# A graph layer with batch and layer norm on one core: another bank for the second half's product, the edges behind x and the weights, one group's low parts by VectorE, high parts two a tile

## The chip, the core and the metric

The kernel runs on one core of a Trainium2 chip. The metric is the device time of one execution in microseconds (us). Before the change three runs took 2590.15, 2593.97 and 2595.03 us, median 2593.97. TensorE (PE) multiplies, its weight loads are listed apart as PEld; VectorE is DVE, ScalarE is ACT, GpSimd is POOL, and SyncE (SP) issues most of the transfers.

## The reference, cut to what matters

x has 50000 rows of 512 numbers; `src` and `dst` list 75000 edges, sorted by `dst`, with every row's loop to itself among them.

```python
summed = segment_sum(x[src], dst, n)
cnt = segment_sum(ones, dst, n)
aggr = summed / maximum(cnt, 1)[:, None]
h = aggr @ W_l.T + b_l + x @ W_r.T
mu = mean(h, axis=0); var = mean(square(h - mu), axis=0)
y = x + relu((h - mu) * rsqrt(var + EPS) * gamma + beta)
out = (y - mean(y, -1)) / sqrt(var(y, -1) + EPS)
```

Since each row has its loop, the kernel computes h as x (W_l + W_r) plus z, where z is the mean over a row's edges of (x of the source minus x of the row), times W_l. Only some rows have edges beside the loop.

## The kernel before, in words

The rows of x come in 78 groups of five tiles of 128 rows (`TG` = 5) and a last one of 80 rows. There are two phases. Phase one computes h, writes it to memory (`h_scratch`) and sums its columns and their squares. Phase two reads h and x again, normalises, and writes `out`.

**A group in phase one.** SP loads the turned x of a group (`raw`, two buffers). The load of group g+2 is issued when PE has finished group g (`after_group`, L377). Each fp32 number is split in two parts, so that three products of reduced precision give the accuracy of fp32: ACT writes the high part (`x_high`, L728, four pieces kc = 0 to 3), POOL or DVE the low part by a subtraction (`x_low`, L1309 on POOL, L1045 on DVE). PE multiplies a tile in 12 matmuls (`product`, L524 to L526) into one of the two banks `pd0`, `pd1`, which take turns. ACT copies a finished tile out of its bank (`copy_h`, L735). So tile t+2 can't begin before tile t is copied.

**The front.** The first 8 groups (`FRONT` = 8) have nothing but plain tiles for PE, while DVE works out from the edges which rows need a correction. PE makes seven sorts of small sums for this between its tiles (the table `between`): `rank_extras` after tile (6, 2), `sum_cover` after (7, 1). Only then is `s_flag` set, which tells every engine whether the edges are of the usual kind. POOL makes all the low parts of the front. In ACT's order a front tile's copy is followed by one piece of the high part of the next group (L766 and on: copy 0, piece 0, copy 1, piece 1 and so on). The first piece waits for `raw`.

**The turns.** Then come 84 turns (u = -2 to 81). Those from 0 to 77 mix a correction for about 256 rows (in two halves h = 0, 1 of 128) with four or five plain tiles; 351 tiles are left for the turns, and the last three corrections have none beside them. PE's order in a turn: spread 0, tile, spread 1, tile, turn 0, tile, turn 1, tile, z of half 0, a fifth tile in about half of the turns, `fill_slots` (23 small matmuls for the turn after next), z of half 1. "Turn h" transposes the differences `dd` into bank `turned[h]`, px for half 0 and p7 for half 1 (`transpose_difference`, L621). ACT and DVE write high and low part from there (`difference_high` L786, `difference_low` L1100), PE multiplies them by W_l into the one bank pz (`correction`, `times_wl`, L627 to L629), ACT copies z to `zz` (`copy_z`, L793), and POOL adds it to `h_scratch` by an indirect transfer (L1379) and then gathers the rows of x for the turn after (L1331). DVE begins the differences when the gathered rows land (L1079). In ACT's and DVE's order stand also the squares and sums of a group three turns back (L799, L1109, L1116).

Each engine works through its own list in order; semaphores tie them together. The wait that guards pz: half 1 of turn u waits for `s_ze` 2u+1, the copy of half 0 just before it.

**The start.** SP issues x of group 0, both weights, x of group 1, three short vectors and a clearing store. ACT issues six small loads of the edges (L745 to L757) on its own queue, before its first activation. PE's first matmul needs the low part of W_l + W_r, which DVE and ACT make once both weights are there (L926, L762, L922).

## Time and profile before

| | |
|---|---|
| runs, us | 2590.15, 2593.97, 2595.03 |
| the profiled execution, us | 2596.68, of which the span of its instructions 2594.9 |
| busy: PE, DVE, ACT, POOL | 1757.6, 1956.6, 1471.8, 1456.2 us |
| mean granted TensorE clock | 0.845 of full speed |
| front, start to the first tile of group 8 | 0 to 156 us |
| turns | 156 to 1840 us |
| last sums and the norm's vectors | to 1883 us |
| phase two | 1883 to 2595 us |

How to read it: times in the rows are microseconds from the span's start. In a timeline row stand start, duration, engine, line, operation, what it writes and reads, how often it is repeated, and in brackets how long the engine was idle before it and what ended that. A merged row (x4) gives the duration of all four. In a row of waits stand who waited for whom, the total, the number and the longest. PE at full clock issues a matmul of 512 columns each 0.23 us, so that a tile takes 2.72 us.

### The profile page before, as it was taken

The page shows a single profiled execution, that of the slowest core. Times are in us where ns is not written, and L with a number is a line of the kernel's source. Part 1 is how long each engine was busy: PE and PEld are TensorE (multiplying, and loading weights), DVE is VectorE, ACT ScalarE, POOL GpSimd, SP SyncE. Part 2 cuts the span into 40 slices and gives each one's busy share as a digit, 9 for nine tenths or more (in the row PEclk, how much of TensorE's full clock was granted, in tenths as well). Part 3 has the DMA queues.
Part 4 walks back from the last instruction along what each step waited for, and adds up shares of the span by engine and source line. Part 5 has one row for each costly group of instructions (what it writes and reads, how often), then busy time and mean ns, then how long its engine had stood idle before and what let it go on. Part 6 is the DMA issues. An engine that isn't in the chain of part 4 may idle for free.

```text
span 2594.9 us, 29629 instructions
## 1 busy us (share of the span) xinstructions
PE 1757.6 (68%) x9404; PEld 1415.7 (55%) x9404; DVE 1956.6 (75%) x3451; ACT 1471.8 (57%) x2847; POOL 1456.2 (56%) x700
## 2 busy tenths in 40 slices
PE   7899999999999999999999999996400000000000
PEld 5778778878877887787778778874200000000000
DVE  6745878888877888888788888785688666666666
ACT  4333455545554554454445445542389988888887
POOL 5354555555555555555565555554196655555564
PEclk9999999999999999999999999997755555555555
DMA  5466878887888878888788878877599999999998
GB/s 184 139 211 206 260 250 266 277 253 246 257 263 255 258 246 259 258 255 264 234 262 271 255 243 253 280 240 247 163 410 426 426 426 426 426 412 414 421 421 344
DMA packets 125533, 752.89 MB, mean 290 GB/s; under 512 B 20809, under 2 KB 20809, under 8 KB 65726
## 3 DMA queue, kind: packets, MB, share of 16 engines
q1 hardware_dynamic: 70464, 617.84, 62.1%
q0 software_dynamic: 53664, 132.51, 20.7%
q8 instruction: 77, 1.26, 0.2%
q10 hardware_dynamic: 1246, 0.60, 0.1%
q14 instruction: 82, 0.67, 0.1%
HBM read 515.32 MB, written 246.22 MB: 293 GB/s over the span
## 4 chain that ended last, share of the span: by engine, by line
PE 33%; DMA 32%; issue 9%; DVE 9%; ACT 8%; POOL 7%; SPq 0%; POOLq 0%; ACTq 0%; DVEq 0%
DMA out<-hx 19%; PE pd L524 7%; PE pd L526 7%; PE pd L525 7%; DMA xn<-x,gi 5%; DMA xf<-x,gi 5%; PE pz L627 3%; PE pz L629 3%; PE pz L628 3%; ACT hx L881 3%; POOL xn L1331 2%; ACT hx L891 2%; DVE x_lo L1045 2%; POOL xf L1331 2%; DMA hs<-h_scratch 1%
## 5 line engine op out<-in xcount | busy, mean ns | idle before, releaser
L524 PE MATMUL pd<-wc_hi,x_hi 128*128 128x512 f32 x1564 | 628.8, 402 | 34.8 <-DVE wc_lo L922 17.3
L1379 POOL DMA_INDIRECT h_scratch<-zz,si x156 | 308.8, 1979 | 564.5 <-ACT zz L793 506.9
L735 ACT ACTIVATE h_out<-pd 128x512 f32<-128x512 f32 x391 | 233.6, 597 | 672.3 <-PE pd L526 652.1
L526 PE MATMUL pd<-wc_hi,x_lo 128*128 128x512 f32 x1564 | 614.6, 393 | 0.0
L525 PE MATMUL pd<-wc_lo,x_hi 128*128 128x512 f32 x1564 | 612.9, 392 | 0.0
L1402 POOL TENSOR_TENSOR hx<-hx,scale_b 128x2560 f32<-128x2560 f32 (+2 forms) x91 | 439.4, 4838 | 293.3 <-DMA hx<-h_scratch 251.8
L524 PEld LDWEIGHTS pd<-wc_hi,x_hi 128*128 128x128 f32 x1564 | 295.4, 189 | 98.5 <-issue 29.9
L526 PEld LDWEIGHTS pd<-wc_hi,x_lo 128*128 128x128 f32 x1564 | 295.2, 189 | 64.7
L525 PEld LDWEIGHTS pd<-wc_lo,x_hi 128*128 128x128 f32 x1564 | 295.9, 189 | 57.9
L1331 POOL DMA_INDIRECT xn<-x,gi x156 | 264.9, 1698 | 47.7 <-issue 47.7
L881 ACT ACTIVATE hx<-hx,nm 128x512 f32<-128x512 f32 x391 | 277.1, 710 | 2.8
L891 ACT ACTIVATE hx<-hx,nr,rs 128x512 f32<-128x512 f32 x385 | 278.6, 798 | 0.0
L627 PE MATMUL pz<-wl_hi,dT_hi 128*128 128x512 f32 x624 | 256.5, 411 | 28.9 <-ACT zz L793 20.3
L1331 POOL DMA_INDIRECT xf<-x,gi x156 | 248.7, 1594 | 47.6 <-issue 47.3
L1079 DVE SCALAR_TENSOR_TENSOR xf<-xn,ndeg,xf 128x512 f32<-128x512 f32 x156 | 114.9, 746 | 185.8 <-issue 140.3
L799 ACT ACTIVATE hs<-hs 128x512 f32<-128x512 f32 x391 | 219.1, 621 | 51.1 <-DVE acc L1109 51.1
L628 PE MATMUL pz<-wl_lo,dT_hi 128*128 128x512 f32 x624 | 247.4, 396 | 0.0
L629 PE MATMUL pz<-wl_hi,dT_lo 128*128 128x512 f32 x624 | 246.4, 395 | 0.0
L728 ACT ACTIVATE x_hi<-raw 128x640 fp32r<-128x640 f32 (+1 forms) x316 | 214.1, 724 | 40.7 <-DMA raw<-xT_whole 40.6
L1109 DVE TENSOR_TENSOR acc<-acc,hs 128x2560 f32<-128x2560 f32 (+1 forms) x79 | 220.1, 2786 | 21.7 <-DMA hs<-h_scratch 21.7
L1116 DVE TENSOR_TENSOR acc<-acc,hs 128x2560 f32<-128x2560 f32 (+1 forms) x79 | 220.2, 2787 | 16.0 <-ACT hs L799 16.0
L1045 DVE TENSOR_TENSOR x_lo<-raw,x_hi 128x640 fp32r<-128x640 f32 x280 | 209.4, 808 | 14.7 <-ACT x_hi L728 14.7
(221 smaller groups left out, 2855.0 us busy)
## 6 DMA issues: line engine op xcount, KB each, us to landing
raw<-xT_whole SPq DMA_DIRECT2D x78, 1280.0 KB
h_scratch<-h_out SPq DMA_DIRECT2D x78, 1280.0 KB
hs<-h_scratch SPq DMA_DIRECT2D x78, 1280.0 KB
hx<-x SPq DMA_DIRECT2D x78, 1280.0 KB, 20.7
hx<-h_scratch SPq DMA_DIRECT2D x77, 1280.0 KB, 15.4
out<-hx SPq DMA_DIRECT2D x77, 1280.0 KB, 18.0
xn<-x,gi POOLq DMA_INDIRECT x156
xf<-x,gi POOLq DMA_INDIRECT x156
```

The costliest lines, as they stand in the source:

```text
L524: pe.matmul(pd[i][0:n, :], hi, wc["hi"][:, kc, :], start=kc == 0, stop=False)
L525: pe.matmul(pd[i][0:n, :], hi, wc["lo"][:, kc, :], start=False, stop=False)
L526: last = pe.matmul(pd[i][0:n, :], lo, wc["hi"][:, kc, :], start=False, stop=kc == KC - 1)
L627: pe.matmul(out_bank[0:n, :], hi, wl["hi"][:, kc, :], start=kc == 0, stop=False)
L628: pe.matmul(out_bank[0:n, :], hi, wl["lo"][:, kc, :], start=False, stop=False)
L629: last = pe.matmul(out_bank[0:n, :], lo, wl["hi"][:, kc, :], start=False, stop=kc == KC - 1)
L881: act.activation(hb[i][0:n, t, :], xb[i][0:n, t, :], ACT.Square, bias=nm2[0:n, k % 4, t:t + 1], accum_out=ssq2[0:n, k % 4, t:t + 1]).then_ ...
L891: act.activation(hb[i][0:n, t, :], xb[i][0:n, t, :], ACT.Identity, bias=nr2[0:n, k % 4, t:t + 1], scale=rs2[0:n, k % 4, t:t + 1]).then_inc ...
L1045: dve.tensor_tensor(x_lo[:, b, kc, 0:n], raw[:, b, kc, 0:n], x_hi[:, b, kc, 0:n].bitcast(F32), ALU.subtract).then_inc(s_xld, 1)
L1331: return pool.indirect_dma_start(out=table if scatter else out, out_offset=by if scatter else None, in_=out if scatter else table, in_offs ...
L1379: pool.indirect_dma_start(out=h_dram[:, :], out_offset=by, in_=zz[:, h, :], in_offset=None, bounds_check=N + 2 * P - 1, oob_is_err=True, c ...
L1402: pool.tensor_tensor(hb[i][0:n, a:b], hb[i][0:n, a:b], scale_b[0:n].unsqueeze(1).to_broadcast([n, b - a, D]), ALU.mult).then_inc(s_mul, 1)
```

## The change

Four edits, with new places for two small steps that hang on the third.

1. The z of half 1 is written to px (`z_to`), which by then has been read by ACT and DVE. Half 1 has no wait for a copy any more, half 0 waits for the copy of half 0 of the turn before, and the transposition of half 0, which writes px, waits for the copy of half 1 of the turn before.
2. The six small loads of the edges are issued by SP, after both weights and ahead of x of group 1.
3. The low parts of group 4 (`MIDDLE`) are made by DVE in the midst of its work on the edges, not by POOL. `rank_extras` stands after tile (5, 3) and `sum_cover` after (6, 1).
4. In the front two pieces of the high part follow each of the copies 0 and 1, instead of one piece each of the copies 0 to 3.

```diff
+MIDDLE = 4
...
+        z_to = (pz, px)
...
         def lo_by_dve(g):
-            return KC * g - KC * FRONT + 1
+            return KC * g - KC * FRONT + KC + 1
+        def lo_by_pool(g):
+            return KC * g + KC - KC * (g > MIDDLE)
...
+            sp.dma_start(src_i[:, :, 0:EB], src.rearrange("(c b p) -> b c p", b=BP, p=EB)).then_inc(s_src, 16)
...
+            sp.wait_ge(s_pad, 1)
+            sp.dma_start(dst_i[:, 1:BC - 1, 0:wide], blocks(BP, [[EB, BP], [lot, BC - 2]])).then_inc(s_dst, 16)
...
             load_xT(1)
...
                 if t == 0:
-                    if isinstance(g, int) and g <= FRONT:
-                        pe.wait_ge(s_xlp, KC * g + (KC if g > 0 else 1))
+                    if isinstance(g, int) and g == MIDDLE:
+                        pe.wait_ge(s_xld, KC + 1)
+                    elif isinstance(g, int) and g <= FRONT:
+                        pe.wait_ge(s_xlp, lo_by_pool(g) if g > 0 else 1)
...
-                (6, 2): (rank_extras,),
-                (7, 1): (sum_cover,),
+                (5, 3): (rank_extras,),
+                (6, 1): (sum_cover,),
...
                 if u > 0:
                     pe.wait_ge(s_dl, 2 * u + h - 1)
+                    if h == 0:
+                        pe.wait_ge(s_ze, 2 * u)
...
                 pe.wait_ge(s_dl, 2 * u + h + 1)
-                if 2 * u + h > 0:
-                    pe.wait_ge(s_ze, 2 * u + h)
-                times_wl(pz, P, h).then_inc(s_z, 1)
+                if h == 0 and u > 0:
+                    pe.wait_ge(s_ze, 2 * u - 1)
+                times_wl(z_to[h], P, h).then_inc(s_z, 1)
...
-                    if g >= 1 and t < KC:
-                        x_high(g + 1, (g + 1) % 2, t)
+                    if g >= 1 and t < KC // 2:
+                        for kc in (2 * t, 2 * t + 1):
+                            x_high(g + 1, (g + 1) % 2, kc)
...
-                act.activation(zz[:, h, :], pz[:], ACT.Copy, scale=wgt[:, u % 4, h:h + 1]).then_inc(s_ze, 1)
+                act.activation(zz[:, h, :], z_to[h][:], ACT.Copy, scale=wgt[:, u % 4, h:h + 1]).then_inc(s_ze, 1)
...
                 dve.scalar_tensor_tensor(vals[a, :, :, k], v, 256.0, vd, ALU.subtract, ALU.mult)
+            for kc in range(KC):
+                x_low(MIDDLE, MIDDLE % 2, kc)
             for k, v in enumerate((dlo, slo)):
...
-            for g in range(1, FRONT):
-                for kc in range(KC):
-                    x_low(g + 1, (g + 1) % 2, kc)
+            for g in range(2, FRONT + 1):
+                for kc in range(KC if g != MIDDLE else 0):
+                    x_low(g, g % 2, kc)
```

The order of ACT before, in groups 0 (its last copies) and 1 of the front (h_out is a tile's copy, x_hi a piece of the next group):

```order
L735 ACTIVATE h_out<-pd 128x512 x2
L728 ACTIVATE x_hi<-raw 128x640
L735 ACTIVATE h_out<-pd 128x512
L728 ACTIVATE x_hi<-raw 128x640
L735 ACTIVATE h_out<-pd 128x512
L728 ACTIVATE x_hi<-raw 128x640
L735 ACTIVATE h_out<-pd 128x512
L728 ACTIVATE x_hi<-raw 128x640
```

and in the changed kernel, at the same place:

```order
L761 ACTIVATE h_out<-pd 128x512 x2
L754 ACTIVATE x_hi<-raw 128x640 x2
L761 ACTIVATE h_out<-pd 128x512
L754 ACTIVATE x_hi<-raw 128x640 x2
L761 ACTIVATE h_out<-pd 128x512 x4
```

Two pieces, not one, stand ahead of the copy of tile 1, and none between the copies of tiles 1 (after its two) and 4.

DVE before, in the work on the edges during group 3 (vals are what the slots are filled from):

```order
L997 TENSOR_TENSOR e_c<-e_a,e_c 125x780
L999 SCALAR_TENSOR_TENSOR vals<-got,e_d 125x780 x2
L1001 TENSOR_TENSOR vals<-got,e_d 125x780 x2
L1002 CAST vals<-e_act 125x780
```

and in the changed kernel:

```order
L1017 TENSOR_TENSOR e_c<-e_a,e_c 125x780
L1019 SCALAR_TENSOR_TENSOR vals<-got,e_d 125x780 x2
L926 TENSOR_TENSOR x_lo<-raw,x_hi 128x640 x4
L1023 TENSOR_TENSOR vals<-got,e_d 125x780 x2
L1024 CAST vals<-e_act 125x780
```

The four subtractions of group 4 have come in between.

SP at the start of the changed kernel (before, L356 for group 1 followed the two weights at once):

```order
L365 DMA raw<-xT_whole 128x2560
L370 DMA w_raw<-wT_l 128x4x512
L370 DMA w_raw<-wT_r 128x4x512
L371 DMA src_i<-src 120x5x125
L379 DMA dst_i<-dst 120x3x127
L380 DMA dst_i<-dst 119x127
L381 DMA dst_i<-dst 119x127
L382 DMA dst_i<-dst 1x126
L383 DMA dst_i<-dst 1x126
L365 DMA raw<-xT_whole 128x2560
```

The load of group 1's x has moved behind six small ones, on the same queue.

## Rows read from the trace of the kernel before

**Rows 1.** Windows of the core: busy PE, PEld, DVE, ACT, POOL; clock, DMA share, GB/s.
```profile
156.00:1750.00 1594.00, 1559.52 (x8541) 1264.16 (x8541) 1270.43 (x1838) 777.87 (x1342) 895.05 (x527) 1.00 0.81 255
...
1883.00:2595.00 712.00, 0.00 (x0) 0.00 (x0) 507.81 (x1416) 595.57 (x1333) 439.10 (x91) 0.50 0.99 414
```

**Rows 2.** Timeline of the start, ACT, DVE and PEld.
```profile
6.62 1.28 ACT L728 ACT_TABLE_LOAD   x1 [6.62 <-issue]
15.08 1.29 DVE L926 TENSOR_TENSOR w_raw<-w_raw 128x512 f32<-128x512 f32 x2 [11.63 <-DMA w_raw<-wT_r]
17.27 0.29 PEld L524 LDWEIGHTS pd<-wc_hi,x_hi 128*128 128x128 f32 x1 [17.27 <-issue]
19.53 2.61 ACT L728 ACTIVATE x_hi<-raw 128x640 fp32r<-128x640 f32 x4
20.74 0.81 DVE L935 CAST srcf<-src_i 120x625 f32<-120x625 int32 x1 [0.39 <-DMA dst_i<-dst]
```

**Rows 3.** DMA, 0 to 33 us: a queue's packets, MB, share; an issue's us to landing.
```profile
q10 hardware_dynamic: 1246, 0.60, 7.6%
...
w_raw<-wT_r SPq DMA_DIRECT2D x1, 1024.0 KB, 13.2
```

**Rows 4.** Timelines round group 4's first tile (DVE's x_lo: a turn); one window last.
```profile
87.17 0.60 ACT L735 ACTIVATE h_out<-pd 128x512 f32<-128x512 f32 x1 [1.49 <-PE pd L526]
98.94 0.60 ACT L735 ACTIVATE h_out<-pd 128x512 f32<-128x512 f32 x1 [11.17 <-PE pd L526]
...
93.42 0.29 PEld L524 LDWEIGHTS pd<-wc_hi,x_hi 128*128 128x128 f32 x1 [6.71 <-POOL x_lo L1309]
...
80.92 12.44 POOL L1309 TENSOR_TENSOR x_lo<-raw,x_hi 128x640 fp32r<-128x640 f32 x4 [19.31 <-ACT x_hi L728]
...
117.97 4.64 POOL L1309 TENSOR_TENSOR x_lo<-raw,x_hi 128x640 fp32r<-128x640 f32 x3 [7.69 <-ACT x_hi L728]
...
76.83 5.47 DVE L999 SCALAR_TENSOR_TENSOR vals<-got,e_d 125x780 bf16<-125x780 f32 x2
...
1010.49 3.02 DVE L1045 TENSOR_TENSOR x_lo<-raw,x_hi 128x640 fp32r<-128x640 f32 x4
...
94.00:99.50 5.50, 5.50 (x15) 4.29 (x13) 5.47 (x9) 0.56 (x2) 0.00 (x0) 0.51 0.46 193
```

**Rows 5.** Timelines of groups 5 to 8, ACT, PEld, POOL; waits of PEld, 17 to 156.
```profile
110.13 0.60 ACT L735 ACTIVATE h_out<-pd 128x512 f32<-128x512 f32 x1 [1.49 <-PE pd L526]
...
117.15 0.74 ACT L728 ACTIVATE x_hi<-raw 128x640 fp32r<-128x640 f32 x1 [3.17 <-DMA raw<-xT_whole]
117.80 0.58 ACT L735 ACTIVATE h_out<-pd 128x512 f32<-128x512 f32 x1
...
124.31 0.60 ACT L735 ACTIVATE h_out<-pd 128x512 f32<-128x512 f32 x1 [1.49 <-PE pd L526]
...
118.43 0.19 PEld L524 LDWEIGHTS pd<-wc_hi,x_hi 128*128 128x128 f32 x1
...
146.95 9.01 POOL L1309 TENSOR_TENSOR x_lo<-raw,x_hi 128x640 fp32r<-128x640 f32 x4 [6.96 <-ACT x_hi L728]
...
156.01 0.19 PEld L524 LDWEIGHTS pd<-wc_hi,x_hi 128*128 128x128 f32 x1 [2.08 <-POOL x_lo L1309]
...
PEld pd L524 <- POOL x_lo L1309: 9.4, 4, 6.7
```

**Rows 6.** The chain that ended last, 235 to 1750 us, by line; PEld's waits there.
```profile
by line: issue 14.1%; DMA xn<-x,gi 9.2%; PE pd L524 8.9%; PE pd L526 8.8%; PE pd L525 8.8%; DMA xf<-x,gi 7.8%; PE pz L627 5.0%; PE pz L629 4.5%; PE pz L628 4.5%; POOL xn L1331 4.0%; DVE x_lo L1045 3.3%; POOL xf L1331 2.8%; DVE hot L1051 1.8
...
PEld pz L627 <- issue: 16.2, 33, 1.6
```

**Rows 7.** Timelines: half 1's copy and the next transposition; the last turn's z.
```profile
479.18 0.67 ACT L793 ACTIVATE zz<-pz,wgt 128x512 f32<-128x512 f32 x1
...
484.95 0.37 PEld L621 LDWEIGHTS px<-ident,dd 128*128 128x128 f32 x2
...
1835.15 0.19 PEld L627 LDWEIGHTS pz<-wl_hi,dT_hi 128*128 128x128 f32 x1 [1.27 <-issue]
```

More of the change, by code:

```diff
@@ L361, in _, with blocks @@
                 sp.dma_start(w_raw[:, m], w.rearrange("(c p) f -> p c f", p=P)).then_inc(s, 16)
+            sp.dma_start(src_i[:, :, 0:EB], src.rearrange("(c b p) -> b c p", b=BP, p=EB)).then_inc(s_src, 16)
+            wide, lot = EB + 2, BP * EB
+            def blocks(first, pattern):
+                return bass.AP(dst.tensor, first * EB - 1, [*pattern, [1, wide]])
+            sp.wait_ge(s_pad, 1)
+            sp.dma_start(dst_i[:, 1:BC - 1, 0:wide], blocks(BP, [[EB, BP], [lot, BC - 2]])).then_inc(s_dst, 16)
+            sp.dma_start(dst_i[1:BP, 0, 0:wide], blocks(1, [[EB, BP - 1]])).then_inc(s_dst, 16)
+            sp.dma_start(dst_i[0:BP - 1, BC - 1, 0:wide], blocks((BC - 1) * BP, [[EB, BP - 1]])).then_inc(s_dst, 16)
+            sp.dma_start(dst_i[0:1, 0, 1:wide], dst[0:EB + 1].rearrange("(o p) -> o p", o=1)).then_inc(s_dst, 16)
+            sp.dma_start(dst_i[BP - 1:BP, BC - 1, 0:wide - 1], dst[E - EB - 1:E].rearrange("(o p) -> o p", o=1)).then_inc(s_dst, 16)
             load_xT(1)
@@ L510, in product @@
                 if t == 0:
-                    if isinstance(g, int) and g <= FRONT:
-                        pe.wait_ge(s_xlp, KC * g + (KC if g > 0 else 1))
+                    if isinstance(g, int) and g == MIDDLE:
+                        pe.wait_ge(s_xld, KC + 1)
+                    elif isinstance(g, int) and g <= FRONT:
+                        pe.wait_ge(s_xlp, lo_by_pool(g) if g > 0 else 1)
                     else:
-                        pe.wait_ge(s_xlp, KC * FRONT + KC)
+                        pe.wait_ge(s_xlp, lo_by_pool(FRONT))
                         pe.wait_ge(s_xld, lo_by_dve(g))
@@ L743, in copy_window @@
                                    banks[a % 3][j][0:EB, 0:HALF], ACT.Copy).then_inc(s_got, 1)
-            act.dma_start(src_i[:, :, 0:EB], src.rearrange("(c b p) -> b c p", b=BP, p=EB)).then_inc(s_src, 16)
-            wide, block = EB + 2, BP * EB
-            def blocks(first, pattern):
-                return bass.AP(dst.tensor, first * EB - 1, [*pattern, [1, wide]])
-            act.wait_ge(s_pad, 1)
-            act.dma_start(dst_i[:, 1:BC - 1, 0:wide], blocks(BP, [[EB, BP], [block, BC - 2]])).then_inc(s_dst, 16)
-            act.dma_start(dst_i[1:BP, 0, 0:wide], blocks(1, [[EB, BP - 1]])).then_inc(s_dst, 16)
-            act.dma_start(dst_i[0:BP - 1, BC - 1, 0:wide], blocks((BC - 1) * BP, [[EB, BP - 1]])).then_inc(s_dst, 16)
-            act.dma_start(dst_i[0:1, 0, 1:wide], dst[0:EB + 1].rearrange("(o p) -> o p", o=1)).then_inc(s_dst, 16)
-            act.dma_start(dst_i[BP - 1:BP, BC - 1, 0:wide - 1], dst[E - EB - 1:E].rearrange("(o p) -> o p", o=1)).then_inc(s_dst, 16)
             for kc in range(KC):
@@ L907, in link, with x_low @@
                 dve.wait_ge(s, steps[s])
+            def x_low(g, b, kc):
+                n = LAST if isinstance(g, int) and g == G else GR
+                dve.wait_ge(s_xh, KC * g + kc + 1)
+                dve.tensor_tensor(x_lo[:, b, kc, 0:n], raw[:, b, kc, 0:n], x_hi[:, b, kc, 0:n].bitcast(F32),
+                                  ALU.subtract).then_inc(s_xld, 1)
             dve.memset(dst_i[0:1, 0, 0:1].bitcast(F32), -1.0)
@@ L1040, in _ @@
             dve.memset(psl[:], 0.0).then_inc(s_ct, 1)
-            def x_low(g, b, kc):
-                n = LAST if isinstance(g, int) and g == G else GR
-                dve.wait_ge(s_xh, KC * g + kc + 1)
-                dve.tensor_tensor(x_lo[:, b, kc, 0:n], raw[:, b, kc, 0:n], x_hi[:, b, kc, 0:n].bitcast(F32),
-                                  ALU.subtract).then_inc(s_xld, 1)
             def one_hots(u):
```

## The prediction

> **What bounds the kernel now.** I read the windows first, to see which engine fills which stage. In the turns PE is busy 1559.5 of 1594 us at full clock; in phase two PE does nothing and DMA is busy 0.99 of the time [rows 1]. Phase two moves the same bytes after the change as before, so it is a block of 712 us that only starts earlier or later. What the change is worth must therefore be read from PE's idle time before 1883 us, and from the end of that stage. Next the waits of PEld (the weight load is the first thing that a stalled PE does not do), which name the two places: 9.4 us for POOL's x_lo in the front [rows 5] and 16.2 us in 33 waits ahead of half 1's z in the turns [rows 6]. Last the chain of waits, which tells whether time won at such a place reaches the end. Between 235 and 1750 us only about 43% of it is PE (26.5% plain tiles, 14% z, small rest); the gathers of xn and xf alone are 17%, and POOL's issuing of them another 7% [rows 6]. So PE is nearly full and yet not the only thing on the path: two chains of about the same length run side by side.
>
> **Part 1, the start (edit 2).** PE's first load is at 17.27, 2.2 us after DVE gets the second weight at 15.08; ACT's table load begins at 6.62, when ACT has issued its last edge load, though nothing it needs is late [rows 2]. The weight takes 13.2 us from issue to landing, and the edges' queue puts 1246 small packets for 7.6% of 33 us, that is 2.5 us of all 16 engines, among the packets of x and weights [rows 3]. About nine tenths of them come before the weight lands; behind it on one queue they cost it nothing, so the weight and with it PE come 2.3 us earlier. The edges land later but have slack: DVE is free for them at 20.35 (20.74 less 0.39 idle) [rows 2], which becomes 18.0. What is late next is x of group 1, now behind the edges. Before, ACT took it up at 19.53 without waiting [rows 2]; with 3.5 us of transfer behind 2.5 us of edges I put it at 19.3 where 17.2 is wanted. Its four pieces (2.61 us) stand in ACT's queue ahead of the copy of tile (0, 0), and PE's third tile waits for that copy: I take 0.5 us. Sum -1.8. From both sides: -3.3 (weights 2.8 earlier and half a microsecond from ACT's table load) to +1.5 (x of group 1 three microseconds late). The Trainium skill, "DMA: Bandwidth & Descriptors", section "Why a DMA increments its semaphore by 16 and not by 1", says that a transfer uses the largest number of engines up to 16 that divides its slowest dimension; for the two loads of 119 rows that is 7 engines, with 34 packets each, against 15 if spread over all. At 32 ns a packet (2.5 us x 16 / 1246) x of group 1 would then come 0.6 us later and the term would be -1.2; no row of this trace tells which engine took what.
>
> **Part 2, group 4 (edit 3).** POOL's four subtractions for group 4 take 12.44 us, against 1.55 each (4.64 for three) where DVE isn't at work on the same memory; DVE's L999 beside them takes 5.47 for two [rows 4]. PE stands 6.7 us, and then runs the tile's rest at half speed: the granted clock from 94 to 99.5 is 0.51 [rows 4]. From one copy to the next pass 98.94 - 87.17 = 11.77 us instead of 2.72: 9.05 us lost in one tile. After the change DVE does the four in 3.02 us [rows 4], POOL does nothing then, and both causes go. The high parts are there by 83.5, so DVE is done by 84.5, and PE wants them at about 87: slack 2.5 us. I take -9.05; the bounds are -9.1 and -6 (if DVE came 3 us too late). DVE's own work is 3 us longer, but L999 and what follows no longer share with POOL, so the marks for `rank_extras` come no later than now; moved to tile (5, 3) it asks for them some 5 us after they are ready.
>
> **Part 3, the front's other groups (edits 3 and 4).** Let T be the end of a group as ACT's copy shows it, which is also when the load of the next x but one is issued. In rows 5 T = 110.13; the first high piece starts at T+7.0 (117.15), the copy of tile 1 at T+7.7 (117.80), PE's fourth tile at T+8.3 (118.43), just when that copy has ended, and the group ends at T+14.2 (124.31). So the fourth tile of a group is already tied to the load. With two pieces ahead of the copy it comes 0.65 us later: fourth tile at T+8.95, end at T+14.8, where five tiles need 13.6. Low parts: first at T+7.8, four of 1.55 us, done at T+14.1, in time. Thus the pairs take away the wait for x_lo at a group's start (0.66 us in rows 5) and put one of about 1.1 us ahead of its fourth tile. I count groups 2 to 6: 5.0 us in all. Then there is the place of the flag. With `sum_cover` after (7, 1), DVE's one-hot tables run beside the low parts of group 8, which take 9.01 us for 6.2 [rows 5]. With it after (6, 1) they run beside those of group 7: +2.8 us, done at T+16.9 where PE wants them at 14.5, a wait of 2.4 us. Against this go the old waits, 9.4 - 6.7 = 2.7 us, and 2.08 us at 156.01 [rows 5]. Sum +2.6; bounds -4.8 (nothing new waits) and +5 (clock at half rate after the 2.4 us wait, which costs up to 1.6 more, and rank_extras late).
>
> **Part 4, the turns (edit 1).** Half 1's z waits in 33 turns, 16.2 us in all, because copy and issue lie between two products in the same bank [rows 6]. This wait goes altogether. What can be late instead: the transposition of half 0 now waits for the copy of half 1 of the turn before. In rows 7 that copy ends at 479.85, the transposition begins at 484.95: 5.1 us of slack, two plain tiles. Behind it on PE would stand everything, so it matters only if it is passed. What is late next is the differences: POOL gathers after adding the turn's last z, 9 to 12 us later DVE can go on, and this loop does not know of pz. Where it is on the chain, a z done sooner only lengthens PE's next wait for DVE. So I take the share of the chain that is PE's, 0.43 of 16.2 = -7.0. Bounds: 0 (all given back) and -17.8 (all kept, and one fall of the clock, 1.6 us, behind the longest wait of 1.6 us saved).
>
> **Part 5, the last turns.** There no tile stands between the halves; the last z of half 1 begins after 1.27 us of waiting at 1835.15 [rows 7], and the last addition, sums and statistics hang on it. -1.2, bounds 0 and -1.6.
>
> **Sum.** -1.8 - 9.05 + 2.6 - 7.0 - 1.2 = -16.4 us. The profiled execution took 2596.7 us (span 2594.9 and 1.8 around it), so 2580.3; it stands 2.7 us above the median of the three runs shown, 2594.0. Against the median I predict 2577.5 us. A change of 0.2% is 5.2 us, about the least that a measurement of this kernel can tell from none.
>
> **The rivals.**
> *The front alone pays.* In the turns the gathers are the bound, part 4 gives 0, the start gives 0.5. For it: the gathers' share of the chain, and that all but the longest of the 33 waits are short, 0.49 us on average, less than the jitter of a gather. Against: PE is busy 98% of the stage. Time: -0.5 - 9.05 + 2.6 - 1.2 = -8.2, 2586.
> *All waits saved are kept, and the pairs cost nothing.* PE's fourth tile finds its copy in time since x lands sooner with PE earlier. -2.5 - 9.05 - 2 - 13 - 1.2 = -27.8, 2566. Against it: the fourth tile is tied to the copy to 0.1 us already [rows 5].
> *The transposition waits (the slower side).* Copy_z of half 1 stands in ACT's list behind the squares of an older group, which wait for DVE's sum, which waits for a load. If this copy came over 5.1 us later than in rows 7 in most turns, PE would stop in all of the 78 turns at a place where it never did. The point from which it decides is 5.1 + 16.4/78 = 5.3 us late; at 5.5 us late 0.4 x 78 = 31 us against 16.4: 2609. For it: ACT's list is in order, and PE now arrives sooner. Against: in rows 7, an instance with squares before the copy, the slack is still 5.1.
> *Group 4 is not repaired:* DVE comes to its four subtractions only after PE wants them, or PE waits as long for the marks at (5, 3). Then part 2 gives 3 instead of 9: 2583 to 2590, within 0.2% only together with part 4 at zero.
>
> **Chances.** Forecast (2571 to 2584) 0.50; front alone (2583 to 2588) 0.22; all kept (2563 to 2571) 0.15; group 4 not repaired 0.08; transposition waits 0.05. Faster by over 0.2% 0.88, within 0.2% 0.07, slower by over 0.2% 0.05. The range for 8 in 10 leaves out the slow rival and the outer part of the two bounds: 2564 to 2589.
>
> **What would show it.** Start: PEld's first load at about 15.0, and ACT's first copy some 0.5 us behind PE's tile. Group 4: no gap near 87 us, clock 1.00 through the front, DVE's four low parts at 3.0 us. Pairs: a wait of PEld for the copy (`h_out`) ahead of fourth tiles, about 1 us in five groups; one wait for x_lo of about 2.4 us at group 7, none at 8; the first tile of group 8 at about 148. Turns: no wait ahead of half 1's z; the waits for DVE's dd and dT_lo larger by some 9 us together; phase two beginning near 1866. I am wrong if waits of PEld appear ahead of the transposition for ACT's zz, if group 4 still waits, or if the turns are not shorter by at least 3 us.

## The result, and the profile after

| Kernel | median us | lowest to highest | runs | against before | 95% interval |
|---|---|---|---|---|---|
| before | 2594.45 | 2590.15 to 2603.87 | 11 | 1 | |
| changed | 2585.88 | 2578.47 to 2589.50 | 11 | 0.9965 | 0.9952 to 0.9977 |

The change makes the kernel 0.35% faster, 8.6 us, with an interval of 6.0 to 12.4 us. Forecast were 16.4 us. The side is right and the time lies in the range, but half of the gain is missing. The changed kernel was timed once more beside the last experiments: 0.9957 (0.9940 to 0.9973), 2585.66 us. The profile of the changed kernel that is read below took 2589.41 us, span 2587.6.

Windows of the changed kernel (busy us of PE, PEld, DVE, ACT and POOL with instruction counts, clock, DMA share, GB/s). The first two answer to [rows 1]; the others are two places in the front that the text comes to below:
```profile
156.00:1750.00 1594.00, 1560.03 (x8584) 1265.86 (x8584) 1274.08 (x1849) 781.92 (x1351) 886.81 (x527) 1.00 0.81 255
1883.00:2587.00 704.00, 0.00 (x0) 0.00 (x0) 502.50 (x1405) 592.45 (x1324) 431.99 (x85) 0.50 0.99 414
...
99.40:102.80 3.40, 3.40 (x10) 2.61 (x9) 3.37 (x3) 1.10 (x2) 3.40 (x3) 0.51 0.00 0
133.50:136.90 3.40, 3.40 (x10) 2.65 (x9) 0.60 (x1) 0.76 (x2) 3.40 (x2) 0.52 0.00 0
```
Phase two is the block that it was (712.4 us before, 712.2 now, from the norm's scale to the end). So the gain must lie ahead of it. A stage is best timed by one recurring instruction; I used the start of ACT's copy of a group's last tile, the first transposition of a turn, and the moment at which the scale for phase two is ready:

| us from the span's start | before | changed | gained so far |
|---|---|---|---|
| group 0 ends | 32.89 | 31.91 | 1.0 |
| group 3 ends | 87.17 | 88.31 | -1.1 |
| group 4 ends | 110.13 | 106.21 | 3.9 |
| group 5 ends | 124.31 | 121.54 | 2.8 |
| group 6 ends | 139.12 | 139.56 | -0.4 |
| group 9 ends | 184.24 | 184.87 | -0.6 |
| turn 0 transposes | 190.86 | 191.48 | -0.6 |
| turn 74 transposes | 1759.66 | 1753.58 | 6.1 |
| scale ready | 1882.55 | 1875.45 | 7.1 |

This is the main reading: the front, from which 8.3 us were expected, gave nothing, and the turns with the last turns gave 7.7, where 8.2 were expected. It is read from one profile of each kernel; how far one profile can be trusted is said ahead of the experiments.

The start, changed kernel (start, us, engine, line, operation, what ended the idle time before it); it answers to [rows 2]:
```profile
0.82 1.28 ACT L754 ACT_TABLE_LOAD   x1 [0.82 <-PEq L1445]
3.19 3.21 SPq L379 DMA_DIRECT2D dst_i<-dst  x1
6.44 2.29 SPq L380 DMA_DIRECT2D dst_i<-dst  x1
15.37 0.29 PEld L548 LDWEIGHTS pd<-wc_hi,x_hi 128*128 128x128 f32 x1 [15.37 <-issue]
```
And the DMA issue of the weight in the first 33 us (KB, us to landing), which answers to [rows 3]:
```profile
w_raw<-wT_r SPq DMA_DIRECT2D x1, 1024.0 KB, 10.8
```
The weight lands in 10.8 instead of 13.2 us and PE begins 1.9 us earlier. Only 1.0 of it is left at the end of group 0. SP itself is busy issuing the edges' loads till 10.44, 5.5 us with two of them, and x of group 1 is issued behind that, at 10.49.

Group 4's first tile, changed kernel, DVE and then ACT; it answers to [rows 4]:
```profile
77.22 5.46 DVE L1019 SCALAR_TENSOR_TENSOR vals<-got,e_d 125x780 bf16<-125x780 f32 x2
82.38 3.14 DVE L926 TENSOR_TENSOR x_lo<-raw,x_hi 128x640 fp32r<-128x640 f32 x4
85.42 5.47 DVE L1023 TENSOR_TENSOR vals<-got,e_d 125x780 bf16<-125x780 f32 x2
...
88.31 0.60 ACT L761 ACTIVATE h_out<-pd 128x512 f32<-128x512 f32 x1 [2.12 <-PE pd L550]
91.03 0.60 ACT L761 ACTIVATE h_out<-pd 128x512 f32<-128x512 f32 x1 [2.12 <-PE pd L550]
```
The repair works: the low parts are there at 85.5, and one copy follows the other by 2.72 us where it was 11.77. DVE's pair at 77.22 takes 5.46 us with POOL idle, and took 5.47 before; but before, it started at 76.83 and POOL's subtractions only at 80.92, so it ran beside them for its last 1.4 us only. The pair that did run beside POOL before is the next one, L1001:
```profile
82.01 7.75 DVE L1001 TENSOR_TENSOR vals<-got,e_d 125x780 bf16<-125x780 f32 x2
```
It took 7.75 us where the changed kernel, with POOL idle, needs 5.47 (L1023). So both engines suffered: POOL's four subtractions took 12.44 us, and DVE lost 2.3 on this pair.

What went wrong is five tiles later. ACT, then PEld, changed kernel, the load of group 5 and PE's fourth tile of group 4; the last row is group 6's fourth tile, with the load of group 7 ([rows 5] has the same places of before):
```profile
96.92 1.36 ACT L754 ACTIVATE x_hi<-raw 128x640 fp32r<-128x640 f32 x2 [5.29 <-DMA raw<-xT_whole]
98.19 0.58 ACT L761 ACTIVATE h_out<-pd 128x512 f32<-128x512 f32 x1
...
98.82 0.19 PEld L548 LDWEIGHTS pd<-wc_hi,x_hi 128*128 128x128 f32 x1 [2.81 <-ACT h_out L761]
...
132.18 0.19 PEld L548 LDWEIGHTS pd<-wc_hi,x_hi 128*128 128x128 f32 x1 [2.55 <-ACT h_out L761]
```
x of group 5 lands 8.6 us after group 3 ended, not 7.0. The pair of high parts and the copy behind it come that much later; PE stands 2.8 us, and 0.7 us after it goes on its clock falls to half for 3.4 us (0.51 in the window from 99.40 above): ten matmuls, where the stretch from 103.0 to 106.4, at full clock, has 16. The same happens at 132.

The largest wait of PEld in the front (17 to 190 us), changed kernel (us in total, times, longest):
```profile
PEld pd L548 <- ACT h_out L761: 10.9, 7, 2.8
```
All seven end before 156 us, the end of the window in [rows 5]; in that window 9.4 us for x_lo have become 10.9 us for the copy.

The turns, changed kernel, 235 to 1750 us: the chain that ended last by line, then the waits of PEld; they answer to [rows 6]:
```profile
by line: issue 13.8%; DMA xf<-x,gi 9.6%; PE pd L548 8.7%; PE pd L550 8.6%; PE pd L549 8.6%; DMA xn<-x,gi 6.4%; POOL xn L1347 4.9%; DVE x_lo L926 3.4%; POOL xf L1347 3.2%; PE pz L653 2.8%; PE pz L654 2.5%; PE pz L655 2.5%; PE px L653 2.1%; P
...
PEld pd L548 <- issue: 17.1, 15, 2.5
PEld px L647 <- DVE dd L1110: 13.4, 11, 2.0
PEld p L647 <- DVE dd L1110: 11.7, 16, 0.8
PEld pz L653 <- DVE dT_lo L1116: 7.9, 20, 0.7
PEld pe L637 <- DVE xe_lo L1100: 7.3, 7, 1.2
```
The wait ahead of half 1's z is gone and there is none for `zz`. The other five were 12.2, 9.9, 11.0, 8.6 and 3.4 us before: they grew by 12.3 us together. The share of PE in the chain is what it was, and the gathers stand on it as before.

### The profile page after: what moved, and what is told of

Read it like the earlier page. It is cut to its first block, busy times and chain, and to the rows that moved or that the text cites. A ratio compares the mean times of both kernels' runs of the same rounds, so it can differ in the third digit from the quotient of the medians.

```text
span 2587.6 us, 29551 instructions
## 1 busy us (share of the span) xinstructions
PE 1753.3 (68%) x9404; PEld 1413.6 (55%) x9404; DVE 1955.3 (76%) x3455; ACT 1471.5 (57%) x2847; POOL 1434.7 (55%) x696
## 4 chain that ended last, share of the span: by engine, by line
DMA 35%; PE 33%; issue 9%; DVE 8%; ACT 7%; POOL 7%; SPq 1%; POOLq 0%; DVEq 0%; ACTq 0%
DMA out<-hx 21%; PE pd L548 7%; PE pd L550 7%; PE pd L549 7%; DMA xf<-x,gi 6%; DMA xn<-x,gi 4%; POOL xn L1347 3%; DMA raw<-xT_whole 2%; ACT hx L895 2%; DVE x_lo L926 2%; POOL xf L1347 2%; PE pz L653 2%; ACT hx L905 2%; PE pz L654 2%; PE pz L655 2%
## 5 line engine op out<-in xcount | busy, mean ns | idle before, releaser
L1347 POOL DMA_INDIRECT xn<-x,gi x156 | 278.3, 1784 | 47.7 <-issue 47.4
L1347 POOL DMA_INDIRECT xf<-x,gi x156 | 235.5, 1510 | 47.5 <-issue 47.5
L926 DVE TENSOR_TENSOR x_lo<-raw,x_hi 128x640 fp32r<-128x640 f32 (+1 forms) x284 | 212.5, 809 | 34.3 <-ACT x_hi L754 34.3
L1347 POOL DMA_INDIRECT xe<-x,gi x78 | 98.3, 1261 | 98.3 <-DVE si L1085 71.1
L1067 DVE TENSOR_TENSOR hot<-iota_b,rel 125x1664 bf16<-125x1664 bf16 x78 | 146.8, 1882 | 1.4 <-issue 1.4
L1259 DVE TENSOR_TENSOR pd<-hx,p 128x512 f32<-128x512 f32 x130 | 88.8, 692 | 61.5 <-POOL hx L1418 60.4
```

Of the source, the lines that this page charges most:

```text
L926: dve.tensor_tensor(x_lo[:, b, kc, 0:n], raw[:, b, kc, 0:n], x_hi[:, b, kc, 0:n].bitcast(F32), ALU.subtract).then_inc(s_xld, 1)
L1347: return pool.indirect_dma_start(out=table if scatter else out, out_offset=by if scatter else None, in_=out if scatter else table, in_offs ...
```

## The experiments

Times carry the ratio to the kernel before, timed on the same chip in the same job. Two places are read from each profile: where group 9 ends (before 184.24, changed 184.87) and how long turns 0 to 74 take (before 1568.8, changed 1562.1). One profile is one sample: the changed kernel run again has 187.91 and 1558.2. Two of the kernels below have the changed kernel's front without a difference, and their group 9 ends at 183.22 (z put back) and 183.15 (gathers first). Of this spread of 4.8 us nearly all arises in group 8, which took 16.35, 18.79, 15.06 and 14.68 us in the four profiles; the end of group 7 agrees within 1.0 us (154.22, 154.83, 153.86, 154.18; before 154.40). So a difference of 3 us at group 9 between two single profiles shows little.

**First, the parts of the change one at a time.**

*Edit 1 alone* (kernel before, half 1's z to px with its waits):
```diff
-                times_wl(pz, P, h).then_inc(s_z, 1)
+                times_wl(z_to[h], P, h).then_inc(s_z, 1)
```


> The kernel before with edit 1 alone (half 1's z in px). If the turns' gain is of this edit alone: turns shorter by 6.7 us (first transposition of turn 0 to that of turn 74), the last turns by 1.0, 2586 to 2588 us, nothing changed up to 156 us. Rival (the gain in the turns comes from where the front leaves the gathers): 2591 to 2595 us.

Measured: 2589.95 us, 0.9989 (0.9977 to 1.0001); turns 1566.7. That is 2.9 us, with an interval from nothing to 6, and the time lies between the two expectations.

*Group 4 alone* (kernel before, its low parts by DVE, all else in place):
```diff
+            for kc in range(KC):
+                x_low(MIDDLE, MIDDLE % 2, kc)
...
-                for kc in range(KC):
-                    x_low(g + 1, (g + 1) % 2, kc)
+                for kc in range(KC if g != MIDDLE else 0):
+                    x_low(g, g % 2, kc)
```


> The kernel before with group 4's low parts by DVE alone (marks and flag at their old places, pieces one a tile, edges by ACT, z in pz). If my term of 9.05 us holds: 2584 to 2587 us, the fifth tile of group 9 copied at 175 to 177 us (before 184.2), clock 1.00 from 20 to 156 us. Rival (what is won at group 4 is lost to late loads and waits for x_lo at groups 5 to 8): 2588 to 2592 us, the fifth tile of group 9 at 179 or later.

Measured: 2588.14 us, 0.9979 (0.9968 to 0.9991), the largest single gain; group 9 ends at 179.47, 4.8 us earlier and not 9, as the rival had it. The clock is 1.00 through the front. Its waits of PEld, 17 to 190 us:
```profile
PEld pd L535 <- POOL x_lo L1322: 5.8, 4, 1.9
PEld pd L535 <- ACT h_out L746: 4.3, 3, 2.6
```
Even with single pieces the copy comes 2.6 us late once, in group 4, and x of group 5 is what ACT waited for:
```profile
95.91 0.74 ACT L739 ACTIVATE x_hi<-raw 128x640 fp32r<-128x640 f32 x1 [5.68 <-DMA raw<-xT_whole]
```

*The start alone* (kernel before, the edges' loads on SP behind x and weights):
```diff
-            act.dma_start(src_i[:, :, 0:EB], src...)
+            sp.dma_start(src_i[:, :, 0:EB], src...)
```


> The kernel before with edit 2 alone (edges by SP behind the weights). By what the changed kernel's trace shows: PE's first weight load at 15.4 us (17.3 before), copy of the last tile of group 0 at 31.9 (32.9 before): of 1.9 us won 0.9 are given back while ACT waits for x of group 1; at 156 us about 1 us earlier. Rival: all 1.9 us kept, which would put the loss in the changed kernel on the pairs.

Measured, one run: 2590.87 us; group 0 ends at 31.2, 1.7 us earlier, and group 9 at 182.74, 1.5 us earlier. Its turns took 1560.8 with z in one bank, 8 us less than those of the kernel before, from which they do not differ, so a single profile doesn't tell the turns to better than 5 to 8 us.

*Group 4 and the pairs* (the kernel of group 4 alone, two pieces ahead of the copies of tiles 0 and 1):
```diff
-                    if g >= 1 and t < KC:
-                        x_high(g + 1, (g + 1) % 2, t)
+                    if g >= 1 and t < KC // 2:
+                        for kc in (2 * t, 2 * t + 1):
+                            x_high(g + 1, (g + 1) % 2, kc)
```


> e4 (group 4's low parts by DVE, all else as before) with edit 4, the pairs behind the copies 0 and 1. Theory P: waits for h_out of 0.9 to 1.4 us at fourth tiles and of 2.5 to 2.8 in groups 4 and 6, where x lands after 9 us, and the clock falls behind those two: fifth tile of group 9 copied at 182 to 186 us (e4 179.5). Rival F (the loss is of the earlier places of rank_extras and sum_cover): within 1 us of e4's 179.5.

Measured, one run: 2594.7 us; group 9 ends at 186.22, 6.75 us later than with group 4 alone. At the end of group 7 it is 3.9 us (154.24 against 150.35); the other 2.9 came in group 8, whose length varied by 4.1 in the changed kernel's front. Expected were 182 to 186. Its waits in the front and the window behind the longest:
```profile
PEld pd L535 <- ACT h_out L746: 10.1, 7, 3.3
...
99.00:103.00 4.00, 3.61 (x9) 2.90 (x10) 3.96 (x3) 2.08 (x4) 4.00 (x3) 0.57 0.01 5
```
The parts of the front add up: 184.24 - 1.5 - 4.8 + 6.75 = 184.7, and the changed kernel has 184.87. With the spread told above, that they meet so closely is luck.

**Second, the changed kernel with other pairs.**

*One piece ahead of each copy again:*
```diff
-                    if g >= 1 and t < KC // 2:
-                        for kc in (2 * t, 2 * t + 1):
-                            x_high(g + 1, (g + 1) % 2, kc)
+                    if g >= 1 and t < KC:
+                        x_high(g + 1, (g + 1) % 2, t)
```


> The changed kernel with one high piece behind each of the copies 0 to 3 of a front tile again (edit 4 undone), all else as changed. Theory P (the pairs are dear): in the trace of the changed kernel PE's weight loads wait 10.9 us in seven waits for the copy h_out, the fourth tile of a group standing behind the copy of tile 1, and twice the clock fell behind it; without the pairs most of this goes: 2577 to 2580 us, the fifth tile of group 9 copied at 176 to 180 us instead of 184.9, waits for h_out under 3 us. Rival L (x lands late): two of the loads took 8.6 us instead of 7.0, because PE now meets them at another time; the pairs are innocent: 2584 to 2587 us, the same falls of the clock at the same groups.

Measured: 2582.80 us, 0.9962 (0.9949 to 0.9976); group 9 ends at 181.56, 3.3 us earlier than in the changed kernel's first profile, half of what the theory wanted; the time lies between the two expectations. The waits (17 to 190 us):
```profile
PEld pd L548 <- ACT h_out L761: 5.2, 4, 2.5
PEld pz L595 <- DVEq L1046: 3.5, 1, 3.5
PEld pd L548 <- POOL x_lo L1324: 2.9, 3, 1.5
```
The second row is new: `rank_extras` at (5, 3) waits for DVE's marks. DVE's nine b_sofar additions take 7.27 us here, beside POOL's low parts of another group, where the changed kernel has 2.08 (row of this kernel, then of the changed one):
```profile
110.94 7.27 DVE L1045 TENSOR_TENSOR b_sofar<-b_sofar,b_member 125x78 bf16<-125x78 bf16 x9
```
```profile
109.81 2.08 DVE L1046 TENSOR_TENSOR b_sofar<-b_sofar,b_member 125x78 bf16<-125x78 bf16 x9
```

*The pairs one tile later:*
```diff
-                    if g >= 1 and t < KC // 2:
-                        for kc in (2 * t, 2 * t + 1):
+                    if g >= 1 and t in (1, 2):
+                        for kc in (2 * t - 2, 2 * t - 1):
```


> The changed kernel with two high pieces behind the copy of tile 1 and two behind that of tile 2 (as in the turns), so that no copy that PE soon needs stands behind a wait for x, and the low parts still start as soon as x lands. Theory P: as e1 or up to 3 us better, 2574 to 2579 us, no wait for h_out in the front at all, short waits for x_lo (under 1 us each). Rival L: 2583 to 2587 us, with the wait now for x_lo where it was for h_out.

Measured: 2582.84 us, 0.9972 (0.9954 to 0.9990); group 9 ends at 179.70, 5.2 us earlier. Waits:
```profile
PEld pd L548 <- POOL x_lo L1325: 8.1, 2, 4.6
...
PEld pd L548 <- ACT h_out L761: 0.6, 1, 0.6
```
The wait for the copy is gone, and two for x_lo stand in its place, as the rival had expected: most of what PE waited for the copy it now waits for the same late x. A second profile of this front (in the last experiment) ends group 9 at 183.58, inside the changed kernel's 183.15 to 187.91. So that the pairs cost time in the front rests on the waits and on the kernels with group 4 alone and with the pairs added; these two kernels point the same way and don't show it by themselves. In whole time neither is told from the changed kernel (2585.88).

*The same, with `rank_extras` and `sum_cover` at their old places, (6, 2) and (7, 1):*
```diff
-                (5, 3): (rank_extras,),
-                (6, 1): (sum_cover,),
+                (6, 2): (rank_extras,),
+                (7, 1): (sum_cover,),
```


> The kernel of e2 (changed kernel, two high pieces behind each of the copies 1 and 2) with rank_extras and sum_cover back after tiles (6, 2) and (7, 1). Theory P (the earlier places are dear too): in e1 PE waited 3.5 us at (5, 3) for DVE's marks, and in e2 8.1 us for x_lo in two waits; at the old places no wait for the marks, x_lo waits as in e4, fifth tile of group 9 copied at 175 to 178 us (e2 179.7), whole 2572 to 2580. Rival F (the places are without effect, only the pairs were dear): 179 to 181 us.

Measured: 2585.31 us, 0.9968 (0.9953 to 0.9983); group 9 ends at 182.45, not at 175 to 178: the theory fell. It is 2.8 us later than in one profile with the early places (179.70) and 1.1 earlier than in the other (183.58), so what the places are worth is not shown.

**Third, why the load comes late.** Eight times, in four profiles (the changed kernel, single pieces, pairs one tile later, group 4 alone), x of group 5 or 7 was taken up 2.04 to 2.06 us after one 16384 byte packet of a queue named "instruction" began. These packets began 6.6 to 7.2 us after the load's issue, and x was taken up after 8.6 to 9.2. Where no such packet fell into the transfer it landed 6.8 to 7.5 us after its issue, in the kernel before too, whose packet of group 7 began only after the landing. (Group 9's load, with a packet 0.7 to 3.1 us after its issue, landed after 7.3 to 7.9 in the same four: a packet near the load's start cost less.) So for group 5 the load was not late before. With edit 1 alone, whose front is that of before, it landed after 6.9 us and the packet began at 9.5. That PE stood at group 4, and so came later to its next instructions, explains this; it is an inference. The repair of group 4 itself moved the packet into the load, from 9.5 to 9.9 us after the issue (three profiles without the repair) to 6.5 to 7.1 (ten profiles with it, that of the next experiment left out). DMA of the changed kernel, 94.8 to 95.2 us (packets, MB, share of 16 engines):
```profile
q8 instruction: 1, 0.02, 14.5%
```
14.5% of 16 engines over 0.4 us is 0.93 us on one engine.

*44 one-column matmuls at the head of PE's program,* so that such packets fall elsewhere (kernel: the one just above):
```diff
+            pe.wait_ge(s_const, 2)
+            for _ in range(44):
+                pe.matmul(p6[0:1, 0:1], ones_b[:, 0:1], ones_b[:, 0:1], start=True, stop=True)
```


> e5 with 44 tiny matmuls more (one column, into a bank nobody uses then) ahead of PE's first product, while PE has nothing to do. Theory I (x lands late when a 16 KB packet of PE's instructions falls into its transfer): in five kernels the x of groups 5 and 7 landed 2.05 us after such a packet began, 8.6 to 9.1 us after the load's issue, all others 7.0 to 7.5. 44 matmuls are 88 instructions, so each packet comes about 10 us earlier in the program: x of groups 5 and 7 lands 7.0 to 7.5 us after the issue, no load of the front later than 7.6 unless a packet falls into it, and the front is 2 to 4 us shorter than e5's. Rival A (the late landing is of the rows of x, or of DVE and POOL at work then): groups 5 and 7 still land 8.6 to 9.1 us after the issue, the front within 1 us of e5's.

Measured: the packets moved from 92.86 and 125.82 to 80.19, 110.64 and 140.98, and x of groups 5 and 7 was taken up 7.3 us after issue both times. The DMA of this kernel, 88 to 96 us, has no instruction packet left, and ACT has its x at 93.14, 1.25 us after it was free, where the kernel without the 44 waited 2.83 till 94.91:
```profile
q1 hardware_dynamic: 268, 2.42, 86.0%
...
93.14 1.37 ACT L757 ACTIVATE x_hi<-raw 128x640 fp32r<-128x640 f32 x2 [1.25 <-DMA raw<-xT_whole]
```
```profile
94.91 1.37 ACT L754 ACTIVATE x_hi<-raw 128x640 fp32r<-128x640 f32 x2 [2.83 <-DMA raw<-xT_whole]
```
So the packet does delay the load. Group 9 ends at 178.96 instead of 182.45, 3.5 us earlier, which agrees with the 2 to 4 expected; 5.1 us of it are there at the end of group 7 (147.33 against 152.43), and 1.6 went again in group 8. It is one profile of each. The Trainium skill ("Runtime: NRT & Kernel Launch", "Instruction fetch mechanics") says that an engine's sequencer fetches its program in blocks of 16 KiB through a DMA queue of its own, and that the cost of passing from one to the next is mostly hidden. The packet's size agrees; hidden it was not, since it was paid by a data load that PE waited for. The whole time is no better (2589.16 us, 0.9974, 0.9960 to 0.9987): this profile's turns took 1576.9 us, the longest of all. Why is not settled.

**Fourth, what edit 1 is worth, and what holds the turns.** Four kernels in one job.

*The changed kernel with z of both halves in pz again:*
```diff
-        z_to = (pz, px)
+        z_to = (pz, pz)
```


> The changed kernel with its turns' z of both halves in pz again, with the waits that go with it: the start, group 4 and the pairs stay as changed. It is meant to be read beside the changed kernel run again in the same job. Theory Z (the whole gain of the change is in the turns, since the front ended 0.6 us later): z in px is worth the 6.7 us that the turns shrank by plus 1.0 after the last turn, so this kernel takes about 7.5 us longer than the changed one, near the kernel before less 1 (2593), and TensorE again waits about 0.43 us in turns before its corrections, 16 to 18 us in all, with the turns taking 1567 to 1569 us. Rival: the waits for pz are largely taken over by the waits for the turned differences and their low parts, as the run with z alone moved suggests (2.9 us shorter than before), and the difference is 3 us (between 0 and 5), near 2589.

*The changed kernel once more:*


> The changed kernel again, as the control of the other three. Both theories: 2583 to 2588 us, turns 0 to 74 in 1557 to 1566 us, the fifth tile of group 9 copied at 183 to 186.5 us.

Measured: 2597.52 us, 1.0005 (0.9987 to 1.0023), against 2585.66 us, 0.9957 (0.9940 to 0.9973). Two things follow. The kernel with all of the front's edits and without edit 1 is no faster than before (the interval leaves at most 3.4 us). And edit 1 is worth 11.9 us by the medians, 12.5 us with 6 either way by the ratios. In the profiles of this pair the turns differ by 7.7 us (1565.9 and 1558.2). The theory's 7.5 us lie within that interval, and the rival's 5 us just outside it. The control's group 9 ended 1.4 us outside what was expected of it: a third fall of the clock, in group 8. The wait is back, a little larger than before, in the kernel with z put back (PEld, 235 to 1750):
```profile
PEld pz L651 <- issue: 19.6, 33, 2.7
```

*The gathers of the next unit ahead of the last z addition* (changed kernel):
```diff
-                    if pair_at(u - 1) is not None:
-                        add_z(u - 1, 1)
                     if pair_at(u + 1) is not None:
                         gather(u + 1, 0)
                     if pair_at(u + 1) is not None:
                         gather(u + 1, 1)
+                    if pair_at(u - 1) is not None:
+                        add_z(u - 1, 1)
```


> The changed kernel with one thing moved: in each turn GpSimd issues the gathers of the next unit before it adds z of the unit before's second half, not behind it. Theory G (the z add holds back the gathers, VectorE's differences of the next unit come late by it, and TensorE waits for them: 24.0 us for the turned differences and 7.3 us for their low parts between 235 and 1750 us): these waits fall to a third, the turns get 12 to 18 us shorter and the kernel takes 2568 to 2575 us. Rival S (the gathers land early anyway and TensorE's waits follow from VectorE's own load): the waits stay within 3 us, and the time is that of the changed kernel within 3 us.

Measured: 2546.55 us (2543.04 to 2546.96, 5 runs), 0.9809 (0.9787 to 0.9831). That is 39 us less than the changed kernel, over twice what the theory gave. The turns take 1517.4 us, 40.8 less than in the changed kernel's profile of the same job. POOL in one turn of the changed kernel: the addition of a unit's last z is 629.74, and all gathers stand behind it and its wait for ACT:
```profile
629.74 1.58 POOL L1395 DMA_INDIRECT h_scratch<-zz,si  x1 [3.27 <-ACT zz L807]
632.41 1.08 POOL L1347 DMA_INDIRECT xe<-x,gi  x1 [1.09 <-DVE si L1085]
...
640.38 1.03 POOL L1347 DMA_INDIRECT xf<-x,gi  x1 [0.30 <-issue]
```
And with the gathers first; the addition of a unit's last z now stands behind them:
```profile
635.21 1.08 POOL L1347 DMA_INDIRECT xe<-x,gi  x1 [2.04 <-DVE si L1085]
...
641.66 3.03 POOL L1347 DMA_INDIRECT xf<-x,gi  x1 [0.30 <-issue]
644.99 1.62 POOL L1395 DMA_INDIRECT h_scratch<-zz,si  x1 [0.30 <-issue]
```
Who waited for the gathers is DVE, ahead of its differences; first the changed kernel, then the one with gathers first (235 to 1750 us):
```profile
DVE xf L1095 <- issue: 123.8, 52, 7.7
DVE xf L1095 <- DMA xf<-x,gi: 37.5, 17, 3.8
DVE xf L1095 <- DMA xn<-x,gi: 8.6, 3, 3.8
```
```profile
DVE xf L1095 <- DMA xn<-x,gi: 7.2, 6, 1.4
DVE xf L1095 <- issue: 1.5, 1, 1.5
```
170 us of waiting have become 9. (The profile names no releaser for the 123.8 us, "issue"; that they too were for the gathers follows from their going when only the gathers were moved.) Nearly all of PEld's waits that came through DVE go with them: of the five in the changed kernel, 57.4 us together, these are left, 16.1 us, with some of the last turns already in the window; the difference is 41 us, as much as the turns lost. And the chain is PE's now (its row is for 235 to 1705 us):
```profile
PEld pe L637 <- DVE xe_lo L1100: 7.2, 8, 1.0
PEld pz L653 <- DVE dT_lo L1116: 4.7, 5, 2.6
PEld p L647 <- DVE dd L1110: 3.4, 1, 3.4
PEld px L647 <- DVE dd L1110: 0.8, 1, 0.8
```
```profile
by line: PE pd L548 16.1%; PE pd L550 16.1%; PE pd L549 16.0%; issue 5.9%; PE px L653 3.7%; PE pz L653 3.5%; PE pz L654 3.4%; PE pz L655 3.4%; PE px L654 3.3%; PE px L655 3.3%; DMA h_scratch<-zz,si 2.7%; DVE x_lo L926 2.5%; DMA xn<-x,gi 2.0
```
The expectation missed the size since it counted only the 31 us of waits for the differences and their low parts, and two thirds of these. Nearly all of them went, and with them the 17.1 us ahead of plain tiles that the waits put down to issue.

*That, and the pairs one tile later:*
```diff
-                    if g >= 1 and t < KC // 2:
+                    if g >= 1 and t in (1, 2):
...
+                    if pair_at(u - 1) is not None:
+                        add_z(u - 1, 1)
```


> The gathers moved as in the run before it, and x_hi's pairs behind the copies of the second and third tile in place of the first and second (the run that did this alone took 2582.8 us). Theory G: 2565 to 2572 us. Rival S: 2582 us within 3. By both, the fifth tile of group 9 is copied at 179 to 182 us, 3 to 5 us before the changed kernel's.

Measured: 2543.87 us (2539.23 to 2546.76, 5 runs), 0.9795 (0.9773 to 0.9818). It is the fastest, 2.05% faster than before, and not to be told from the kernel just above. In its profile group 9 ends at 183.58, against 183.15 above, where 179 to 182 were expected; the waits for x_lo (7.6 us in two) stand where the waits for the copy were.

## Why the prediction was half right, point by point

- **What bounds it.** Right: phase two stayed a block of 712 us, and two chains run side by side in the turns. I named the gathers' chain and used it only to discount part 4; the run with the gathers first shows that it was worth 39 us by itself.
- **Part 1, the start, -1.8.** Right in direction: PE's first load at 15.37 (15.0 forecast), then -1.0 at the end of group 0 in the changed kernel, and -1.7 there and -1.5 at group 9 with this edit alone (all profiles: group 0 ends at 32.3 to 32.9 without this edit, 31.1 to 32.0 with it). SP spends 5.5 us on issuing two of the edges' loads before x of group 1, a cost that the term had left out; that ACT took this x up at 19.37, where 19.3 was forecast, is therefore luck. The -1.2 that was worked out beside it from the Trainium skill ("DMA: Bandwidth & Descriptors", "Why a DMA increments its semaphore by 16 and not by 1") lies as near to what was measured, but no run here tells how many engines took these loads.
- **Part 2, group 4, -9.05.** The step from one copy to the next, 11.77 to 2.72, held to the hundredth. The term didn't. The group took 22.96 us before, 17.90 in the changed kernel and 16.06 with this edit alone, so 5.1 and 6.9 are left of 9.05; alone, another 2.1 went by group 9. The rest was given back five tiles later, where x of group 5 comes late: a wait of 2.8 us with a fall of the clock, or one of 2.6 without. Before, this x had no packet in its way: the packet began 9.9 us after the issue, as told above, and ACT took x up only at 99.44. The stall was priced without asking what else moves when it goes. And the reading that DVE's L999 ran beside POOL's subtractions was wrong; it was L1001 that did, and lost 2.3 us by it.
- **Part 3, the pairs, +2.6.** The failed step. "The fourth tile comes 0.65 us later, a wait of about 1.1 us in each of five groups" is right for the 0.65 us where x lands near T+7.0 (groups 1, 2 and 3 grew by 0.64, 0.73 and 0.75 us, and by 0.56 to 0.62 from the kernel with group 4 alone to that with the pairs added). In group 6, and hidden in group 4's balance, x lands 8.6 to 8.75 us after T, the wait is 2.5 to 2.8, and 3.4 us at half the clock cost 1.7 more: group 6 took 18.02 for 14.81. The sum over groups 1 to 3 and 5 to 9 is +6.7, and over groups 1 to 3 and 5 to 7, where four profiles of this front agree, +5.6 to +6.1, outside the bound of +5. Not all of it is the pairs': with group 4 alone the same groups up to 7 already grew by 2.8, and the pairs added 1.9 there (4.1 with group 4). I made T+7.0 a constant. Five of the other loads in the trace of before would not have warned: they were taken up at T+7.0 to T+7.3. What could have warned was the instruction packet that began 0.07 us after x of group 7 was taken up there. What delays the load is this packet, as the 44 extra matmuls showed.
- **The place of the flag.** Forecast was a wait of 2.4 us at group 7 against 2.08 saved at group 8. No such wait is in the trace. The low parts of group 7 were done at T+17.0, as forecast (16.9), but PE, held up by the late x of that very group, didn't ask for them before T+18.0. Group 7 took 0.6 us less and group 8 0.8 more; what the places are worth by themselves no run here tells.
- **Parts 4 and 5, the turns, -7.0 and -1.2.** As forecast: -6.7 and -1.0 in the first pair of profiles. The reason given, a share of the chain, is not proved by that, and the number is partly luck: over all profiles turns 0 to 74 took 1560.8 to 1568.8 us in five kernels with one bank for z, and 1558.1 to 1576.9 in seven profiles with two banks and the gathers in their old place. From the runs the edit is worth 12.5 us with 6 either way inside the changed kernel, and 2.9 (0 to 6) alone. The first interval contains the 8.2 forecast, the second ends 2 us short of it, and they don't agree well with each other. Whether it is worth more once group 4 and the start are changed is open. The waits for the turned differences and their low parts grew by 3.5 us, not 9; the rest of the growth, to 12.3, is in waits that I hadn't named.
- **The rivals.** "The front alone pays" is the reverse of what happened: the turns alone paid. That its time, 2586, is the one measured is luck. No transposition waited for `zz`. Group 4 was repaired.

## What to carry to other kernels

Before a stall is priced, list what moves when it goes: here the next block of PE's own instructions was fetched 3 us sooner after the load's issue and fell into the load, and with the copy behind it and the clock behind a short wait this took half of 9 us. A landing time that all instances in a trace agree on is still no constant: look at what passed close by it on the same DMA engines. And when a share of the chain belongs to an engine that issues gathers in program order, look at what stands ahead of them in its list: here one addition moved behind the gathers was worth over four times the change under study.

## What the runs showed of the hardware that I had not expected

- A single 16 KB packet of the "instruction" kind held one DMA engine for 0.93 us, and a 1.25 MB load into which it fell 6.6 to 7.2 us after the issue was taken up after 8.6 to 9.2 us, where it was 6.8 to 7.5 without one. Where a packet began 0.7 to 3.1 us after the issue, the load landed after 7.3 to 7.9.
- Two waits of PE of 2.8 and 2.5 us were each followed, 0.7 and 1.4 us after PE went on, by 3.4 us at half the clock, and so in the three other profiles of the same front; with one of 2.6 us, in the kernel with group 4 alone, the clock stayed at 1.00.
- SP took 3.21 and 2.29 us to issue two loads of 0.2 MB or less, and 0.40 for one of 1.25 MB. It is not the loads' form alone: in the kernel before, ACT issued the same two in 0.35 and 0.38 us, and took 2.36 for the third. What held the issuing engine is open.
- Where POOL and DVE work on SBUF, the on-chip memory, at the same time, either or both can suffer: POOL's four subtractions took 12.44 us for group 4 before, and 6.14 for group 8 in the changed kernel; DVE's pair L1001 beside them 7.75 us, and 5.47 with POOL idle; DVE's nine additions 7.27 us beside POOL, and 2.08 without.
